# Two score products of a head group moved from slots 4 and 5 to slots 0 and 1, in three cross-attention steps of four

## The reference

```
x   = layernorm1(tgt);  result = tgt + proj(causal_self_attention(x))
xq  = layernorm2(result);  xs = layernorm2(src)             # src: (8, 750, 512)
k2, v2 = split(xs @ ed_wkv);  q2 = xq @ ed_wq
wei2   = softmax(q2 @ k2^T * scale)                         # (8, 16, 224, 750)
result = result + (wei2 @ v2) @ ed_wproj + ed_bproj
result = result + relu(layernorm3(tgt) @ ff_w1 + ff_b1) @ ff_w2 + ff_b2
```

## Time and profile before

| | |
|---|---|
| median of 3 runs | 1387.36 us (1386.01 to 1387.64) |
| the profiled execution's own time | 1388.35 us |
| its span | 1386.5 us |
| TensorE clock granted, mean | 0.985 of full speed |
| PE busy | 1319.9 us, 95% of the span |
| DVE, ACT, POOL busy | 61%, 47%, 46% |

### The profile page before, as it was taken

The page is one execution under the profiler, slowest core; times in us unless marked ns, Lnnn a source line. Parts: engine busy times, 40 slices in busy tenths (PEclk is TensorE's granted clock), DMA queues, the critical chain, the costliest instruction groups (busy, mean ns, idle before and its releaser), DMA issues.

```text
span 1386.5 us, 24323 instructions
## 1 busy us (share of the span) xinstructions
PE 1319.9 (95%) x9129; PEld 1071.1 (77%) x9129; DVE 838.8 (61%) x2056; ACT 654.9 (47%) x1574; POOL 633.8 (46%) x493
## 2 busy tenths in 40 slices
PE   6999999999899999998799999999999999999998
PEld 6888888888788888886677787777777777787764
DVE  6613223242677676776556758677685867757565
ACT  4311101241656566655526455464645646355344
POOL 3232221232445466556652555555555555545451
PEclk9999999999899999999899999999999999999999
DMA  7400102125834566545278566666657657655641
GB/s 240 141 16 16 61 31 84 38 60 123 176 86 123 153 137 135 138 126 159 78 143 131 103 92 121 89 120 95 95 105 105 117 83 115 102 94 73 93 67 41
DMA packets 98262, 142.22 MB, mean 103 GB/s; under 512 B 9597, under 2 KB 62629, under 8 KB 98146
## 3 DMA queue, kind: packets, MB, share of 16 engines
q1 hardware_dynamic: 98146, 140.67, 50.3%
HBM read 59.40 MB, written 22.02 MB: 59 GB/s over the span
## 4 chain that ended last, share of the span: by engine, by line
PE 75%; DVE 7%; POOL 5%; issue 4%; ACT 4%; DMA 3%; SPq 1%; POOLq 0%; ACTq 0%; DVEq 0%
PE ps L1641 19%; PE ps L452 10%; PE ps L422 10%; PE ps L163 9%; PE ps_pair L1658 6%; PE ps L1673 6%; PE ps L1687 5%; PE ps L1741 4%; DVE ca_xT L1629 2%; DVE ca_maxes L1576 1%; DMA sa_K_stack<-sa_rows 1%; ACT ca_xT_f L1563 1%; POOL sa_rows L154 1%; PE ps L1705 1%; POOL sa_fin L1001 1%
## 5 line engine op out<-in xcount | busy, mean ns | idle before, releaser
L1507 POOL TENSOR_TENSOR ca_partial<-ca_partial,ca_probT 125x896 f32<-125x896 f32 x118 | 251.7, 2133 | 216.7 <-ACT ca_probT L1524 212.1
L1524 ACT ACTIVATE ca_probT<-ps_pair 125x448 f32<-125x448 f32 x384 | 210.7, 552 | 207.2 <-PE ps_pair L1658 206.0
L1576 DVE TENSOR_REDUCE ca_maxes<-ps 112x1 f32<-112x375 f32 x512 | 253.6, 540 | 85.7 <-PE ps L1673 84.9
L1673 PE MATMUL ps<-ca_k_stack,ca_q_stack 96*112 96x376 f32 x512 | 173.0, 367 | 15.8 <-DVE ca_maxes L1576 14.5
L1658 PEld LDWEIGHTS ps_pair<-ca_q_stack,ca_k_stack 98*125 98x125 f32 x768 | 131.0, 187 | 54.1 <-issue 41.1
L311 POOL TENSOR_TENSOR ff_hT<-ff_hrelu,ff_hT 128x512 fp32r<-128x512 f32 (+1 forms) x64 | 77.9, 1218 | 203.0 <-DVE ff_hT L393 203.0
L1658 PE MATMUL ps_pair<-ca_q_stack,ca_k_stack 98*125 98x224 f32 x768 | 163.5, 295 | 2.3 <-ACT ca_probT L1524 2.2
L1641 PE MATMUL ps<-ca_xT,w_a 128*128 128x376 f32 x768 | 157.8, 343 | 0.0
L422 PE MATMUL ps<-ff_w,ff_hT 128*128 128x512 f32 x672 | 155.5, 390 | 0.0
L1641 PE MATMUL ps<-w_b,ca_xT 128*125 128x512 f32 x576 | 152.0, 400 | 0.7 <-DVE sa_res L1128 0.5
L422 PEld LDWEIGHTS ps<-ff_w,ff_hT 128*128 128x128 f32 x672 | 125.6, 188 | 25.8
(11 more groups left out here) (137 smaller groups left out, 2360.1 us busy)
## 6 DMA issues: line engine op xcount, KB each, us to landing
ca_k_stack<-ca_keys SPq DMA_DIRECT2D x96, 376.0 KB, 8.0
sa_Q_stack<-sa_rows SPq DMA_DIRECT2D x96, 112.0 KB, 3.5
sa_K_stack<-sa_rows SPq DMA_DIRECT2D x96, 112.0 KB, 3.8
ca_q_stack<-q_out SPq DMA_DIRECT2D x96, 112.0 KB, 9.5
ctx_tokens<-in_ctx_dram SPq DMA_DIRECT2D x14, 750.0 KB
ctx_tokens<-in_L_xattn_ff_w_dram SPq DMA_DIRECT2D x16, 512.0 KB, 4.5
q_out<-sa_yT SPq DMA_DIRECT2D x16, 448.0 KB, 4.0
ff_xin<-in_x_dram SPq DMA_DIRECT2D x7, 512.0 KB, 3.9
```

The lines of the kernel that those rows point to most:

```text
L1507: pool.tensor_tensor(total, total, half(a), ALU.add).then_inc(partial_done, 1)
L1524: act.activation(probT[u // GH][0:JT, u % GH].rearrange("p a t -> p (a t)"), ps_p[u % 2][0:JT, 0:2 * T], ACT.Exp).then_inc(exp_done, 1)
L1576: dve.tensor_reduce(maxes[:, q, j, a:a + 1], ps_s[n % 3][0:TQ, 0:JH], AX_X, ALU.max).then_inc(s_read, 1)
L1673: pe.matmul(ps_s[n % 3][0:TQ, 0:JP], q_stack[0:KS, h, TQ * q:TQ * (q + 1)], k_stack[0:KS, h, a, :], start=True, stop=True).then_inc(s_psum, 1)
```

## The change

Scores are placed by two tables. `EARLY_SCORES`, for steps with g = 0, 2 and 3, puts one product each in slots 0 and 1, none in slots 2 and 3, one each in slots 4 and 5 and two each in slots 6 to 11, that is in ten of the twelve slots. `LATE_SCORES`, for g = 1, is the old placing. In a slot the first product stands ahead of the filling and a second behind it, as before. So in 24 of the 32 groups two products change places against everything else: slots 4 and 5 have one fewer each, slots 0 and 1 one more each. The other line drops entries from the tail of the list that were already placed in self-attention; both lists have the same 2959 entries, so it drops nothing that would have stood twice.

```
-    return items + [("ca",) + o for o in other[start:]]
+    return items + [("ca",) + o for o in other[start:] if o not in early]
...
+LATE_SCORES = (0, 0, 0, 0, 0, 2, 4, 6, 8, 10, 12, 14, 16)
+EARLY_SCORES = (0, 1, 2, 2, 2, 3, 4, 6, 8, 10, 12, 14, 16)
+SCORED = (EARLY_SCORES, LATE_SCORES, EARLY_SCORES, EARLY_SCORES)
...
-            if 0 <= s - 1 < NG and 4 <= i:
-                scores = [("score", s - 1, 2 * (i - 4) + a) for a in range(2)]
+            if 0 <= s - 1 < NG:
+                scores = [("score", s - 1, u) for u in range(SCORED[g][i], SCORED[g][i + 1])]
```

## The result

| | before | after |
|---|---|---|
| median, us | 1386.8 (1386.01 to 1388.64, 6 executions) | 1410.85 (1405.55 to 1414.54, 6 executions) |
| ratio of after to before | | 1.0175, 95% interval 1.0157 to 1.0194 |
| profiled execution, us (its span) | 1388.35 (1386.5) | 1405.55 (1403.8) |
| mean granted TensorE clock, profiled execution | 0.985 | 0.983 |

The change costs 24 us. The prediction said 1402 us with a range of 1394 to 1408: the sign was right, the size was not, and the time lies above the range. The profiled execution is the shortest of the six, so its trace shows less of the loss than the median does. Medians and ratios in this text are of fast executions alone; two of `begin`'s six, of 1487.5 and 2136.5 us at a mean granted clock of 0.84 and 0.56, are left out.

A forecast was written before the change was run, and what follows sets the result against it. PE, busy for 95% of the span, was taken as the bound. Waits of 20.15 us against 9.9 + 0.35 gained gave +9.9, the clock +5.5: 1401.9 from the 1386.5 us span, stated as 1402 us, range 1394 to 1408.

The forecast's parts named there:

- the net of the waits: Over all changed steps: new waits of 20.15 us against 9.9 + 0.35 gained, so 9.9 us slower.
- Sum of the waits: New PE waits for loads in steps 2, 3, 6, 7, 31, 32 and five with g = 3: 20.15 us.
- gained: Waits that go in g = 2, g = 0 and steps 2 and 32, 9.9 us, plus 0.35 in step 4.
- The waits for queries: First score of a group waits for late loads: 2.7 us step 2, 5.05 step 3, 1.15 g = 3, 2.85 step 32.
- Rivals D (loads in time): Queries land in time, no new wait comes and the gains stand alone: 1377 us, chance 0.04.
- E (half of the waits): Half of the waits, all gains and no lower clock: within 0.2%, chance 0.03.
- The wait in g = 3's slot 10: PE's 1.00 us wait behind a 1.44 us VectorE instruction, held by POOL's timing, was to stay.
- rival B: The wait in g = 3 goes too, six or seven steps gain 1.0 to 1.2 us: 1394 us, chance 0.08.
- I take 0.85: Steps with g = 0: the wait in slot 7 goes, 0.85 us gained per step, from 0.65 to 0.9.
- 2.2 us for two and a half of the three: Half clock behind the long waits of steps 2, 3 and 32: 5.5 us in all, ends nothing and 10 us.
- Rival A: Waits as in the forecast, but PE's short runs between them keep the clock: 1397 us, chance 0.20.
- Rival C: More half clock or late loads; a stretch behind each second of seven shorter waits, 8 us more: 1411 us, chance 0.07.

The follow-up runs named there:

- begin: The kernel after with its new table in steps 2 to 8 alone, LATE_SCORES in steps 9 to 34: 1400.4 us, ratio 1.0097.
- fill: The kernel after with unused products on PE ahead of the first score in steps 2, 3, 6, 32 and those with g = 3: 1408.7 us, ratio 1.0153.
- regular: The kernel after with its new table in steps 9 to 30 alone, the old placing in all others: 1391.05 us, ratio 1.0028.
- three: The kernel after with its new table in steps 2, 3 and 32 alone, the old placing in all others: 1401.09 us, ratio 1.0109.
- again: The kernel after run a second time, unaltered: 1410.72 us, ratio 1.0172.
- threefill: New table in steps 2, 3 and 32 alone, with 12, 22 and 12 unused products on PE ahead of their first scores: 1397.15 us, ratio 1.0076.
- queries: The kernel after with a group's query loads issued ahead of the key copies, not behind them: 1395.43 us, ratio 1.006.
- slots23: The kernel after with the first two products of EARLY_SCORES in slots 2 and 3 instead of 0 and 1: 1382.35 us, ratio 0.9961.
- zero: EARLY_SCORES only behind a batch's fourth group (steps 12, 16, 20, 24, 28), every other step as before: 1384.31 us, ratio 0.9982.
- best: Steps 9 to 30 alone: EARLY_SCORES for g = 2, first two products in slots 2 and 3 for g = 0, the rest as before: 1380.49 us, ratio 0.9957.
- end: The kernel after with its new table in steps 31 and 32 alone, the old placing in all others: 1391.93 us, ratio 1.0041.
- best2: From step 4 on: EARLY_SCORES for g = 2, first two products in slots 2 and 3 for g = 0, the rest as before: 1381.05 us, ratio 0.9963.

## Why the prediction missed

The terms of its sum against the two profiled executions, in us. "Steps" are differences between the step lengths of the two traces, the lower clock included.

| term | predicted | steps |
|---|---|---|
| step 2 | +2.5 | +4.5 |
| step 3 | +5.05 | +7.0 |
| step 4 | -1.2 | -1.2 |
| steps 6 and 7 | +2.3 | +2.6 |
| g = 2, steps 10 to 30 | -2.4 | -1.6 |
| g = 0, steps 8 to 28 | -5.1 | -1.6 |
| g = 3, steps 11 to 27 | +5.75 | +7.2 |
| steps 31 and 32 | +3.05 | +3.0 |
| clock, all together | +5.5 | in the rows above |
| sum | +15.4 | +20.0 |

The two spans differ by 17.3 us only, because the trace of after is 2.7 us ahead when step 2 starts (724.51 against 727.24 us). Nothing changed up to there, so this is no gain of the change.

Three of the rows hold a difference of clock. In step 2 there are 3.4 us of dense half clock more, which cost an estimated 1.7 us, half of their length. In step 3 there are 6.8 us more, which cost 1.8 (`fill`). In step 4 there are 3.4 us less, worth 0.9: with the old row, step 4 takes 22.1 us with 6.8 us at half clock (before) and 21.2 with 3.4 (`regular`, `three`). That leaves 20.0 - 1.7 - 1.8 + 0.9 = 17.4 us of waits at like clock, where the prediction's net was 9.9, and 24 - 17.4 = 6.6 us of clock in the median, where it took 5.5. The lines of `again` say the same: 19 us more at half clock, at 0.29 to 0.39 us each, are 5.5 to 7.3 us.

**The failed step is the net of the waits, 9.9 us: "Sum of the waits" against "gained".** It was 17.4 us. The waits for queries were right, the gains were sized too large, and late loads were put at nothing. The parts follow.

**The waits for queries: right.** Landing time, place and length of each came out nearly as worked: 2.7 us in step 2 (2.99 in the row), 5.05 in step 3 (4.72), 1.15 in g = 3 (1.17 by the step lengths), 2.85 in step 32 (2.71). With the clock kept full, step 3 is 24.5 us in `fill` and in `threefill`, 5.1 more than before: the term to 0.1 us. `queries` confirms the cause, and that the order on SP's queue made it. One thing is luck: step 2's 2.7 us hold for executions with 6.8 us at half clock at the end of step 1, as the trace of before happens to have; with less, the wait was 4.0 us (`three`). Rivals D (loads in time) and E (half of the waits) fail at this.

**The wait in g = 3's slot 10 stayed, as predicted** (rival B falls). PE in step 11, to be held against the earlier trace rows:

```profile
933.35 0.43 PE L1676 MATMUL ps<-ca_k_stack,ca_q_stack 96*112 96x376 f32 x1 [1.01 <-DVE ca_maxes L1579]
```

**First and largest part: "I take 0.85" for g = 0.** The wait in slot 7 went, as said. But the first product, now in slot 0, meets a VectorE that is behind at the end of g = 3. PE at the start of step 16, and VectorE there, whose pair of reductions PE waits for (with POOL's sum, for the last section):

```profile
1020.62 0.38 PE L1661 MATMUL ps_pair<-ca_q_stack,ca_k_stack 98*125 98x224 f32 x2
1021.32 0.40 PE L1676 MATMUL ps<-ca_k_stack,ca_q_stack 96*112 96x376 f32 x1 [0.33 <-DVE ca_maxes L1579]
1021.56 1.88 PE L1744 MATMUL ps<-ca_wp,ca_oT 128*112 128x512 f32 x4
```

```profile
1020.19 0.53 DVE L1632 TENSOR_TENSOR ca_xT<-ca_xT_f,ca_xT 128x375 fp32r<-128x375 f32 x1
1020.64 0.99 DVE L1579 TENSOR_REDUCE ca_maxes<-ps 112x1 f32<-112x375 f32 x2
1020.65 4.43 POOL L1510 TENSOR_TENSOR ca_partial<-ca_partial,ca_probT 125x896 f32<-125x896 f32 x2 [1.71 <-ACT ca_probT L1527]
1021.55 1.58 DVE L1632 TENSOR_TENSOR ca_xT<-ca_xT_f,ca_xT 128x375 fp32r<-128x375 f32 x1
```

From the prob at 1020.62 to the projection (L1744) at 1021.56 are 0.94 us. The same place in `slots23`, where no score stands there:

```profile
1007.01 0.38 PE L1661 MATMUL ps_pair<-ca_q_stack,ca_k_stack 98*125 98x224 f32 x2
1007.22 1.88 PE L1744 MATMUL ps<-ca_wp,ca_oT 128*112 128x512 f32 x4
```

0.21 us. So 0.73 us come in slot 0; 0.17 of it is the product, which slot 4 or 5 no longer has, and 0.55 is a wait. The step gains 0.25 us instead of 0.85; in `zero` as well (0.25), while `slots23` and `best` show 0.8. The term was 5.1 us for six steps and is 1.6: 3.5 us lost. The prediction checked the first product's loads in every step and its reader in none.

**The other gains.** In step 4, 1.2 us were expected and 0.3 came at like clock (20.87 us against 21.18 in `regular`, both with 3.4 us at half clock): the wait in slot 7 was replaced by one of 0.72 us behind VectorE's 0.76 us for the context load. In `queries`, where VectorE does not wait for that load, the step is 19.99 us. In g = 2, 0.4 us were expected and 0.33 came.

**Late loads had no term.** The query loads of step 19 were 1.3 us late, in both executions of the kernel after and in `regular`: +1.2 us. Those of step 14 cost 0.4 us. The prediction knew of such a load (group 14, 10.8 us in the trace of before) and left it to a rival.

**The clock, 5.5 us: the size was about right, the working was not.** "2.2 us for two and a half of the three" waits came out at 6.6 us (5.5 to 7.3 by the lines), inside its own 2 to 10. But the cost does not hang on a wait alone. The wait in step 32 (2.3 to 2.7 us) has none, 3.4 or 6.8 us of half clock behind it (after, `end`, `three`), and steps 6 and 19 had a stretch in one run each (`best2`, `regular`). The profiled execution has 48 us at half clock, where the median one has 58, and the kernel before 41 in its own: the cost is a draw, to be given by its spread over executions and not by one trace. Rival A, no lower clock, fails. The Trainium skill (TensorE: Matmul & The Clock Gate, Part 1: The HAM clock gate (the "warmup" mystery)) has the clock fall behind an idle stretch. The traces agree for step 3, with 4.72 us idle and 6.8 us at half clock. For idle times of 2.2 to 2.7 us the rows alone decide, and they show both outcomes.

**Rival C** had more lower clock and a late load in it, at a chance of 0.07, and its 1411 us is what was measured. That is luck. Its 8 us stood on stretches behind every second short wait (seven by its count, eight by the prediction's list), and the kernel after has none behind any of them (granted clock 1.00 in the windows of steps 6, 7 and 11, and in those of 15 to 31). The difference lay in the net of the waits instead.

In one line: +9.9 of waits was 17.4 in truth (of the difference, 3.5 are g = 0, 1.6 late loads, 0.9 step 4, 0.4 g = 2, the rest small terms), and +5.5 of clock was 6.6; together they are the 24 measured. The split into 17.4 and 6.6 is uncertain by about 1 us.

**What stays open.** Why one group's last query load is late in the regular batches, and which: it is group 18 in the kernel after, 14 before, and 26 in `fill`, where step 19 is on time (22.05 us) and step 27 takes 23.27. And why the context load of step 4 takes 22.5 us in `fill`, 21.2 in the kernel after and at most 21.9 before. Neither was tried by itself.

## What to carry to other kernels

A product moved ahead to help an engine has two things to be checked in its new place: when its inputs land, counted from the transfer's place on its queue, and whether the buffer it writes is free there, that is how far behind its reader is at the end of the step before. Here slot 0 against slot 2 decides between 1.7% slower and 0.4% faster. Compare steps of two traces only where they have the same time at half clock; a step that shrank may only have had less of it. And where dense PE work gets a wait of 2 us or more, price the clock by many executions: one profile may show none of it.

## What was new about the hardware

- The three query loads of group 10 take 2.3 to 2.5 us when issued ahead of the key copies (`queries`) and 9.4 to 10.2 us behind them; group 18 takes up to 10.7 us (10.9 in `regular`), at the same place in three executions.
- A wait of the same length and place (2.3 to 2.7 us, step 32) was followed by 6.8, 3.4 or 0 us at half clock in three kernels with the same table there. In `again` the long stretch of step 3 began at 748.5, inside the wait, as in the kernel after.
- Time at half clock cost 0.29 us per us over 49 executions of before and 0.39 over ten of after.
- Products without use in a wait kept the clock full: step 3 at 1.00 for 24.5 us in `fill` and `threefill`, against 0.87 for 26.3 without them. In step 2, where they left 2.6 us idle, 3.4 us at half clock followed in both.
- A VectorE instruction with two SBUF inputs (L1632) took 1.58 us beside POOL's sum and 0.53 ahead of it, 1.4 us apart (above, 1021.55 and 1020.19; the sum starts at 1020.65).
